# A decoder kernel: the work between the recurrence and block 4, by pairs of batches

## The reference, cut to what matters

```python
# block 3: a gated recurrence, 1024 channels, then a mix back to 256
aiv = x @ W_aiv
a_proj, i_proj, v = jnp.split(aiv, 3, axis=-1)
a = jax.nn.sigmoid(a_proj + decay_bias)
i = jax.nn.sigmoid(i_proj)
input_signal = jnp.sqrt(jnp.maximum(1.0 - a * a, 1e-08)) * (i * v)
h = _chunked_scan(a, input_signal)      # h[t] = a[t] * h[t-1] + input_signal[t]
x = x + h @ W_mix + b_mix
# block 4: cross attention, 16 heads of 16, on a second layer norm
q = _split_heads(query @ Wq.T + bq)     # query = layernorm(x)
scores = jnp.einsum('bhtd,bhsd->bhts', q, k) * scale
attn = jax.nn.softmax(jnp.where(mask[:, None, None, :], scores, -jnp.inf), axis=-1)
out = jnp.einsum('bhts,bhsd->bhtd', attn, v)
x = x + out @ Wo.T + bo
# block 5: one ternary matmul
```

## Time and profile before

| | us |
|---|---|
| median of 3 runs | 472.68 (469.56 to 478.15) |
| profiled execution, its own time | 468.59 |
| its span | 466.8 |
| PE busy | 405.1 |
| DVE busy | 265.4 |
| ACT busy | 162.6 |
| POOL busy | 130.4 |
| aiv projections (L1193) end | 299.7 |
| last state made | 317.3 |
| mix ends | 330.1 |
| first maxima of block 4 | 346.2 |
| first score of batch 0 | 359.8 |
| first score of batch 1 | 370.7 |

### The profile page before, as it was taken

The page is one execution under the profiler, slowest core; times in us unless marked ns, Lnnn a source line. Parts: engine busy times, 40 slices in busy tenths (PEclk is TensorE's granted clock), DMA queues, the critical chain, the costliest instruction groups (busy, mean ns, idle before and its releaser), DMA issues.

```text
span 466.8 us, 7332 instructions
## 1 busy us (share of the span) xinstructions
PE 405.1 (87%) x2920; PEld 266.2 (57%) x2920; DVE 265.4 (57%) x481; ACT 162.6 (35%) x334; POOL 130.4 (28%) x174
## 2 busy tenths in 40 slices
PE   1999977967999986399799999998839999999976
PEld 1556644535467765397555555576513666676655
DVE  5058567996023652012738569985639677677323
ACT  0440530002443133132343554240312566566740
POOL 4720049231763006603550000000162033330100
PEclk9999999986999989589999999999975899999999
DMA  7992003000112796422100000156241333330002
GB/s 232 385 255 92 1 4 93 0 0 1 48 49 69 224 372 276 122 83 62 45 1 0 2 0 0 46 154 159 58 142 53 108 100 98 99 100 2 4 1 70
DMA packets 30616, 42.17 MB, mean 90 GB/s; under 512 B 4330, under 2 KB 27286, under 8 KB 30186
## 3 DMA queue, kind: packets, MB, share of 16 engines
q1 hardware_dynamic: 28279, 35.95, 25.2%
q0 software_dynamic: 2304, 5.76, 4.7%
HBM read 33.00 MB, written 8.98 MB: 90 GB/s over the span
## 4 chain that ended last, share of the span: by engine, by line
PE 67%; DVE 12%; DMA 6%; ACT 5%; POOL 4%; issue 3%; SPq 2%; DVEq 0%; ACTq 0%; POOLq 0%
PE banks L1193 14%; PE banks L951 5%; PE banks L1259 5%; PE banks L1299 4%; PE banks L1006 4%; PE banks L1286 4%; PE banks L991 4%; PE banks L980 3%; PE banks L1227 3%; DVE RA L449 3%; PE banks L940 2%; DMA RC<-NT 2%; PE banks L1031 2%; PE banks L1112 2%; PE banks L1130 2%
## 5 line engine op out<-in xcount | busy, mean ns | idle before, releaser
L1604 DVE TENSOR_REDUCE NM<-banks 100x2 f32<-100x722 f32 x64 | 57.2, 906 | 27.3 <-PE banks L1259 26.2
L1193 PE MATMUL banks<-XT,RBG 128*128 128x400 f32 x192 | 66.7, 510 | 2.1 <-ACT XT L744 2.1
L1193 PEld LDWEIGHTS banks<-XT,RBG 128*128 128x128 f32 x192 | 37.1, 194 | 30.8 <-issue 2.9
L598 POOL TENSOR_TENSOR rstd<-ve,mhalf 100x4 f32<-100x4 f32 x12 | 12.6, 1052 | 140.9 <-DVE ve L1359 140.9
L744 ACT ACTIVATE XT<-banks 128x800 f32<-128x800 f32 x14 | 11.6, 838 | 98.5 <-PE banks L940 98.5
L899 ACT ACTIVATE CT<-banks 128x400 f32<-128x400 f32 (+1 forms) x72 | 35.8, 504 | 26.1 <-PE banks L1286 24.5
L940 PE MATMUL banks<-identf,XN 100*128 100x100 f32 x112 | 15.9, 298 | 19.3 <-DVE XN L1364 9.9
L1259 PE MATMUL banks<-RBG,RC 97*100 97x361 bf16 x64 | 20.9, 425 | 8.1 <-DMA RC<-q_parts 6.6
L1079 PE MATMUL banks<-RC,SELT 128*128 128x400 f32 x64 | 24.6, 534 | 2.7 <-DVE RC L1445 2.4
L940 PEld LDWEIGHTS banks<-identf,XN 100*128 100x128 f32 x112 | 13.8, 169 | 22.6 <-issue 10.6
L1405 DVE TENSOR_TENSOR RC<-RV 128x800 f32<-128x800 f32 x16 | 15.3, 1004 | 17.1 <-ACT RV L786 14.7
(11 more groups left out here) (228 smaller groups left out, 809.6 us busy)
## 6 DMA issues: line engine op xcount, KB each, us to landing
RA<-in_L_ffn_W SPq DMA_DIRECT2D x2, 2048.0 KB, 12.4
k_parts<-RA SPq DMA_DIRECT2D x18, 180.5 KB, 3.4
RBG<-in_L_attn_W_aiv SPq DMA_DIRECT2D x1, 3072.0 KB
CT<-in_ctx_t SPq DMA_DIRECT2D x2, 1444.0 KB, 11.3
RC<-q_parts SPq DMA_DIRECT2D x12, 200.0 KB, 3.7
RBG<-k_parts SPq DMA_DIRECT2D x12, 180.5 KB, 3.6
RA<-k_parts SPq DMA_DIRECT2D x12, 180.5 KB, 3.8
RBG<-k_parts POOLq DMA_DIRECT2D x12, 180.5 KB, 3.7
```

The costliest lines, as they stand in the source:

```text
L1193: ins = mm(PS[2 * aiv_pair(i) + g][:, 0:GC], WA[:, k, c:c + P], XT[:, k, GC * g:GC * g + GC], start=(k == 0), stop=(k == KT - 1))
L1604: v.tensor_reduce(NM[:, b % 2, 2 * i:2 * i + 2], PP[w % 2][0:T, :, 0:S], AX.X, ALU.max, negate=True).then_inc(mx_out, 1)
```

## The change

- **Roots by pairs.** ACT takes roots after every second group; DVE makes a state two groups behind (`inputs(j - 2)`), and two states are left after the loop.
- **The mix by pairs of batches.** A pair's sums lie in one bank. PE runs all eight groups for pair 0, then pair 1 (with pair 0's transposes and query matmuls inside), then pair 2. Pair 3's eight steps (`mix_last`) go into ticks 0 to 14 of block 4.
- **Layer norm, queries, stores and loads by pairs** (`ln_add`, `ln_norm`, `x_tr`, `x_out`, `q_mm`, `q_out`, `queries_through`): pair 0 before block 4, the rest of pairs 1 to 3 in ticks 3 to 26. DVE splits pair 0's queries, POOL those of the other three.
- **Places.** Pair 0's rows lie in RA behind the decays, the other three in RC; SP waits for the whole mix only before these. Query parts and the float32 queries have two buffers each, used in turn.
- The wait of the last squares for old states remains in the text (`u_done, j - 3`), and the semaphores are counted by pair.

The diff, cut to its core (left out: semaphore declarations, counts that follow from them, and the helpers' changed indices):

```diff
-QS = part(RC, 0, G, H, GC, dt=BF16)
+QS = [part(RA, 6500, H, QC, dt=BF16)] + [part(RC, 1600 * i, H, QC, dt=BF16) for i in range(NQ - 1)]
+MIX_BANK = (6, 7, 4, 5)
+TR_BANK = (0, 2, 4, 4)
+Q_BANK = (1, 7, 7, 4)
 P4 = [part(CTF, 1600 * i, H * T) for i in range(3)] + [
     part(SELT[:].rearrange("p a b -> p (a b)"), 0, H * T)]
-QW = part(CTF, 4800, KT, GC)
-QP = part(WX[:].rearrange("p a k d -> p (a k d)"), 0, 3, KT, GC, dt=BF16)
+QW = [part(CTF, 4800 + 400 * i, KT, QC) for i in range(2)]
+QP = [part(WX[:].rearrange("p a k d -> p (a k d)"), 600 * i, 3, KT, QC, dt=BF16) for i in range(2)]
...
+ONCE = ([("mix_last", 2 * j, j) for j in range(RT)]
+        + [("q_mm", 3, 1), ("q_out", 4, 1), ("ln_norm", 5, 2), ("x_tr", 9, 2), ("x_out", 10, 2),
+           ("q_mm", 13, 2), ("q_out", 14, 2), ("ln_add", 15, 3), ("ln_norm", 18, 3), ("x_tr", 23, 3),
+           ("x_out", 24, 3), ("q_mm", 25, 3), ("q_out", 26, 3)])
+ORDER = ("q_mm", "x_tr", "x_out", "q_out", "ln_add", "ln_norm", "parts", "sums_tr", "normalise", "out_tr", "out_mm", "maxima", "scores", "weighted",
+         "os_evac", "add", "mix_last")
...
+            for n, at, x in ONCE:
+                if n == name and name in own and tick == at:
+                    own[name](x)
...
+    def query_ones(p, n):
+        q = QS[p][ROW_MASK:ROW_MASK + 1]
+        if n > 1:
+            q = RC[ROW_MASK:ROW_MASK + 1, 0:1600 * n].bitcast(BF16)
+        else:
+            q = q.rearrange("p h n -> p (h n)")
+        sp.dma_start(q, ones_d.rearrange("a b -> (a b)").unsqueeze(0)[:, 0:H * QC * n]
+                     ).then_inc(qs_one[min(p, 1)], 16)
+    def queries_through(p):
+        sp.wait_ge(q4_first, p + 1)
+        store_queries(p, 0)
+        for i in (1, 2):
+            if p == 0:
+                sp.wait_ge(q4_split, i)
+            else:
+                sp.wait_ge(q4_split1, 2 * (p - 1) + i)
+            store_queries(p, i)
+        for i in range(3):
+            load_queries(sp, p, i)
...
+    query_ones(0, 1)
+    queries_through(0)
     sp.wait_ge(y_mm, 3 * B)
-    sp.dma_start(QS[ROW_MASK:ROW_MASK + 1].rearrange("p g h n -> p (g h n)"),
-                 ones_d.rearrange("a b -> (a b)")[0:H * N].unsqueeze(0)).then_inc(qs_one, 16)
-    for i in range(3):
-        if i == 0:
-            sp.wait_ge(q4_out, 2)
-        else:
-            sp.wait_ge(q4_split, i)
-        store_queries(0, i)
-    for i in range(3):
-        load_queries(sp, 0, i)
+    query_ones(1, NQ - 1)
+    queries_through(1)
     for b in range(B):
         sp.wait_ge(np_out, b + 1)
         for i in range(3):
             load_maxima(sp, b, i)
-        if b == 0:
-            for i in range(3):
-                sp.wait_ge(q4_split1, max(i, 1))
-                store_queries(1, i)
-            for i in range(3):
-                load_queries(sp, 1, i)
+        if b + 2 < NQ:
+            queries_through(b + 2)
...
-    rsqrt(4)
-    pool.wait_ge(q4_out, 4)
-    link(gp.tensor_tensor(QW, QW, QP[:, 0], ALU.subtract))
-    gp.tensor_copy(QP[:, 1], QW).then_inc(q4_split1, 1)
-    pool.wait_ge(q4_split1, 1)
-    gp.tensor_tensor(QP[:, 2], QW, QP[:, 1], ALU.subtract).then_inc(q4_split1, 1)
-    bias(4)
+    def rsqrt_pair(p):
+        pool.wait_ge(var4, p + 1)
+        gp.tensor_tensor(rstd[:, 2 * p:2 * p + 2], ve[:, 2 * p:2 * p + 2], mhalf[:, 0:2], ALU.pow
+                         ).then_inc(rstd4, 1)
+    def split_query(p):
+        qw, qp = QW[p % 2], QP[p % 2]
+        pool.wait_ge(q4_out, p + 1)
+        link(gp.tensor_tensor(qw, qw, qp[:, 0], ALU.subtract))
+        gp.tensor_copy(qp[:, 1], qw).then_inc(q4_split1, 1)
+        pool.wait_ge(q4_split1, 2 * p - 1)
+        gp.tensor_tensor(qp[:, 2], qw, qp[:, 1], ALU.subtract).then_inc(q4_split1, 1)
+    for p in range(3):
+        rsqrt_pair(p)
+    split_query(1)
+    rsqrt_pair(3)
...
+        if b == 0:
+            split_query(2)
+            split_query(3)
+            bias(4)
...
-        if j % 4 == 3:
-            for jj in range(j - 3, j + 1):
+        if j % 2:
+            for jj in (j - 1, j):
...
+    def x_out(p):
+        act.wait_ge(tr4, p + 1)
+        src = PS[TR_BANK[p]][:, 0:KT * QC].rearrange("p (k n) -> p k n", k=KT)
+        sc.activation(XT[:, :, QC * p:QC * p + QC], src, ACT.Copy).then_inc(xt4, 1)
+    def q_out(p):
+        qw, qp = QW[p % 2], QP[p % 2]
+        act.wait_ge(q4_mm, p + 1)
+        if p >= 2:
+            for i in range(3):
+                act.wait_ge(q_st[i], 16 * (p - 1))
+            if p == 2:
+                act.wait_ge(q4_split, 2)
+            else:
+                act.wait_ge(q4_split1, 2 * (p - 2))
+        for m in range(KT):
+            q = PS[Q_BANK[p]][:, QC * m:QC * m + QC]
+            ins = sc.activation(qp[:, 0, m], q, ACT.Identity, bias=BQ4[:, m:m + 1], scale=1 / 4)
+        ins.then_inc(q4_first, 1)
+        for m in range(KT):
+            q = PS[Q_BANK[p]][:, QC * m:QC * m + QC]
+            ins = sc.activation(qw[:, m], q, ACT.Identity, bias=BQ4[:, m:m + 1], scale=1 / 4)
+        ins.then_inc(q4_out, 1)
+    x_out(0)
+    q_out(0)
+    x_out(1)
...
-    pe.wait_ge(iv_done, RT)
-    pe.wait_ge(sig, 2 * RT)
     pe.wait_ge(ld["wmix"], 16)
-    for j in range(RT // 2):
+    def mix(p, j):
         pe.wait_ge(state, j + 1)
-        for b in range(B):
-            mm(PS[b][0:T, 0:D], UU[:, j, b, 1:TP], WMIX[:, j, :], start=(j == 0), stop=False)
-    for b in range(B):
-        for j in range(RT // 2, RT):
-            pe.wait_ge(state, j + 1)
-            ins = mm(PS[b][0:T, 0:D], UU[:, j, b, 1:TP], WMIX[:, j, :], start=False,
-                     stop=(j == RT - 1))
-        ins.then_inc(y_mm, 1)
-    pe.wait_ge(x_new, 3 * B + 6)
-    for i in range(4):
-        g, m = i // 2, i % 2
-        if m == 0:
-            transposes(4 * B, g)
-        pe.wait_ge(xt_ready, 4 * KT * G + KT * (g + 1))
-        if i >= 2:
-            pe.wait_ge(q4_out, i - 1)
-        for k in range(KT):
-            ins = mm(PS[4 + m][:, 0:GC], W4[:, 2, k, m * P:(m + 1) * P], XT[:, k, GC * g:GC * g + GC],
-                     start=(k == 0), stop=(k == KT - 1))
+        for b in (2 * p, 2 * p + 1):
+            ins = mm(PS[MIX_BANK[p]][0:T, b % 2 * D:b % 2 * D + D], UU[:, j, b, 1:TP], WMIX[:, j, :],
+                     start=(j == 0 and b % 2 == 0), stop=(j == RT - 1), skip_group_check=True)
+            if j == RT - 1:
+                ins.then_inc(y_mm, 1)
+    def x_tr(p):
+        if p == 0:
+            pe.wait_ge(sig, 2 * RT)
+        elif p == 1:
+            pe.wait_ge(iv_done, RT)
+        elif p == 3:
+            pe.wait_ge(xt4, 3)
+        for b in (2 * p, 2 * p + 1):
+            pe.wait_ge(xn_ready, 4 * B + b + 1)
+            for k in range(KT):
+                t0 = QC * k + b % 2 * T
+                ins = nc.tensor.transpose(PS[TR_BANK[p]][:, t0:t0 + T], XN[:, b, k * P:(k + 1) * P],
+                                          identf[0:T, 0:T])
+        ins.then_inc(tr4, 1)
+    def q_mm(p):
+        pe.wait_ge(xt4, p + 1)
+        if p == 1:
+            pe.wait_ge(x_new, 3 * B + 4)
+        elif p == 2:
+            pe.wait_ge(q4_out, 2)
+        for m in range(KT):
+            for k in range(KT):
+                ins = mm(PS[Q_BANK[p]][:, QC * m:QC * m + QC], W4[:, 2, k, m * P:(m + 1) * P],
+                         XT[:, k, QC * p:QC * p + QC], start=(k == 0), stop=(k == KT - 1))
         ins.then_inc(q4_mm, 1)
-    pe.wait_ge(x_new, 4 * B)
-    pe.wait_ge(pv_zero, 1)
+    pe.wait_ge(sig, 2 * RT - 1)
+    for j in range(RT):
+        mix(0, j)
+    for j in range(RT):
+        mix(1, j)
+        if j == 4:
+            x_tr(0)
+        if j == 6:
+            q_mm(0)
+    pe.wait_ge(iv_done, RT - 1)
+    for j in range(RT):
+        mix(2, j)
+    x_tr(1)
...
+            pe.wait_ge(q4_out, 3)
...
-        if j >= 4:
-            inputs(j - 4)
+        if j >= 2:
+            inputs(j - 2)
...
-    for j in range(RT - 4, RT):
+    for j in range(RT - 2, RT):
         inputs(j)
-    for b in range(B):
-        add(3, b, PS[b])
-    dve.wait_ge(x_new, 4 * B)
-    dve.wait_ge(q4_out, 2)
-    link(v.tensor_tensor(QW, QW, QP[:, 0], ALU.subtract))
-    v.tensor_copy(QP[:, 1], QW).then_inc(q4_split, 1)
+    def ln_add(p):
+        both = (2 * p, 2 * p + 1)
+        dve.wait_ge(y_mm, 2 * B + 2 * p + 2)
+        if p == 0:
+            dve.wait_ge(bias_added, 3)
+        for b in both:
+            v.tensor_tensor(X[:, b], X[:, b], PS[MIX_BANK[p]][0:T, b % 2 * D:b % 2 * D + D], ALU.add
+                            ).then_inc(x_new, 1)
+        for b in both:
+            stats(4, b)
+        for b in both:
+            aggregate(4, b)
+        dve.wait_ge(aggregated, 4 * B + 2 * p + 2)
+        v.tensor_scalar(ve[:, 2 * p:2 * p + 2], mv[:, 2 * p:2 * p + 2, 1], EPS, None, ALU.add
+                        ).then_inc(var4, 1)
+    def ln_norm(p):
+        dve.wait_ge(rstd4, p + 1)
+        for b in (2 * p, 2 * p + 1):
```

(14 more changed lines are left out.)

86 lines of the change are left out of this document (45 added, 41 removed).

## The result

The changed kernel takes **482.4 us** (median of 4 runs, 481.5 to 486.7) against 472.3 for the kernel before on the same chip (4 runs, 469.6 to 478.2): ratio 1.0235, 95% interval 1.016 to 1.031. The forecast was 468.7, in a range of 462.5 to 474.5, so the prediction was wrong in sign and outside its range.

A forecast was written before the change was run, and what follows sets the result against it. It took PE, busy 87% of the span, as the bound, with slack only in the passage from recurrence into block 4. -6.1 + 1.7 + (0 to 1.9), taken as -4.0, gave 468.7 against the 472.68 median; range 462.5 to 474.5.

The forecast's parts named there:

- States and roots: Recurrence: last state at 310.2 instead of 317.3, 7.1 us earlier; four more table loads covered by the projections.
- The first fall: PE thin from 304.2 to 311.1 during pair 0's mix: half clock afterwards costs 1.7 us.
- Pair 0's queries: Pair 0's layer norm, queries, split and DMA before block 4: first maxima at 329.3 instead of 346.2.
- the row's midpoint: Landing of pair 0's last 100 KB query load: midway between 1.7 and 3.84 us, taken as 2.8.
- The SP rival: Four store and load rounds in SP's queue, 2 us more per store under key loads: 472.7, no change; chance 0.17.
- Pair 3's mix and the first score: Start of block 4: pair 3's mix done at 343.1, first score at 353.1 against 359.8, -6.7 us.
- Batch 0: POOL's splits and bias precede batch 1's maxima: batch 1's first score at 364.6 instead of 370.7, gain 6.1 us.
- the second fall: PE thin from 343.1 to 353.1: half clock doubles pair 3's transposes and query matmuls, 0 to 1.9 us.
- The clock term: Two thin PE stretches, 304.2 to 311.1 and 343.1 to 353.1: +1.7 and 0 to 1.9 us.
- The slower rival: Clock stays low after the first gap, over 10.5 us of fp32 work from pair 0's query wait: 480.7; chance 0.08.
- Within: 0.89: Chance given to a whole-kernel result within 2% (9.5 us) of the kernel before.

The follow-up runs named there:

- e4: Kernel before with only roots by pairs and states two groups behind: ratio 1.0036.
- e1: Changed kernel with POOL's block 4 bias moved behind the split of batch 1's maxima: median 473.8 us.
- e3: Changed kernel with 7 and 6 idle fp32 matmuls before batch 7's last transposes and last output product: median 475.8 us, ratio 1.0134.
- e9: e6's kernel with POOL's key loads issued ahead of the split of the maxima: median 464.5 us, ratio 0.980.
- e2: Changed kernel with 28 small idle fp32 matmuls on PE right before its wait for batch 1's split maxima: median 478.8 us.
- e8: e7 plus two idle fp32 matmuls of 400 columns ahead of each of pair 0's mix steps 6 and 7: ratio 0.998, median of all 475.1 us.
- e12: Kernel before with 7 repeated copies (2.0 us) on POOL ahead of batch 3's split of the maxima: 475.5 us, ratio 1.005.
- e7: e6's kernel plus 22 idle fp32 matmuls ahead of PE's wait before the first score: median 478.7 us, ratio 1.012.
- e10: Kernel before with POOL's key loads issued ahead of the split of the maxima: ratio 0.999.
- e6: Changed kernel with the edits of e1 and e3 together: median 471.3 us of six runs, ratio 0.986.

## Why the prediction was wrong, point by point

- **States and roots: right.** The last state ended at 310.80 (310.2 forecast), and the loads cost nothing (e4). PE waited 0.78, 1.66 and 0.74 us for states, and the last step of pair 0 began at 310.84.
- **The first fall: right in place and size.** Clock 0.50 from 308 to 312; PE's 24 records from 310.84 on took 7.16 us, where 20 had taken 4.48 at full clock: 1.8 us more, 1.7 forecast.
- **Pair 0's queries: 2.7 us too early.** First maxima at 331.98, not 329.3. The chain shows the reason:

```profile
322.24 4.14 DMA q_parts<-WX
326.40 0.59 SPq L430
...
329.57 2.27 DMA RA<-q_parts
```

  The store took 4.14 us from ScalarE's result until the loads could go, while the key loads still kept the DMA engines 0.76 busy (322 to 326); I had given split, issue and landing together 2.0. The landing of the last load (2.27, forecast 2.8) was well bounded: of the two readings, the row's midpoint was too high by 0.5. The other, the estimate of 2.9 from the fixed cost of a DMA in the Trainium skill (DMA: Bandwidth & Descriptors, "Anatomy of one DMA"), was too high by 0.6. The SP rival had this mechanism, but 2 us are its whole part.
- **Pair 3's mix and the first score: 2.5 us late in all.** Last mix step to 344.6 (343.1), first score at 355.61 (353.1). The gain there was 4.2 instead of 6.7.
- **Batch 0, the step that failed.** I had the wait: "adds the bias, 4.49 us, all ahead of batch 1's maxima", through at 360.7; it was 363.57, as pair 3's mix ended 1.5 us late and the second fall, which I had in the sum, slowed its queries. I priced it as a wait, the difference between 364.6 and 362, and went on at full clock: "After that the order is the old one." What came was a stop of 2.90 us, then 24 us at half clock. Batch 1's first score stood at 371.16, 6.6 us behind the forecast (2.9 from POOL, 3.7 from PE's now slow way from the split to the score), and its sums 21.9 us after that instead of 14.6 before. e1 shows what the wait is worth: without it 10 us come back in the profile, and 8.6 in the median of all runs (482.4 to 473.8, with 472.3 and 473.5 for the kernel before beside them). It is not the only thing that can start this fall (e3, e9).
- **The clock term.** I looked for falls in the two stretches that are thin *because of the change's mix*, found both (308 to 315, 348 to 355) and priced each by the work *inside* the thin stretch, 1.7 and 0 to 1.9 us. The third thin place, PE's idle time from 360.7 to 363.6, I had worked out myself (362 to 364.6 at the score) and didn't put into this list. And a fall is priced by what is behind it until the clock is back: 24 us of block-4 work, half of it lost, 12 us against my forecast at full clock.
- **The slower rival was the right mechanism in the wrong place.** It kept the clock low on the moved fp32 matmuls, 327.6 to 338, and gave 480.7; there the clock stayed at 1.00. It stayed low on block 4's matmuls behind the bias instead. My argument against it, "packed fp32 matmuls brought it back within 3.5 us", is true of such matmuls (e2: back within 3 us of the fill's start). It doesn't carry over to block 4's mix of small ones, behind which the clock was back after 7 us in e2, e8 and e12, but after 17 in e7 and 27 here. The row that did say it was in my hands: 345 to 365 at 0.50 with PE 17.32 of 20 us busy. I used it as the rival's price and gave it 0.08.
- **The steady part and the tail: not in the forecast.** +1.5 us from PE's three waits for the maxima rows (2.0 us), which go away with the key loads out of their way (e9). Why they are longer than before's one wait of 0.54 us, with the same loads in the same order, is open: the landings were 4.2 to 4.4 us against 3.9 to 4.1. +4.3 us from a fall at 461, at waits that before has too; e4 has it as well, and e10 and e12 in part. That fall is a matter of the execution, not of the change alone: nothing in these runs ties it to the change.
- **The scatter.** "Within: 0.89" rested on it that the change can do no more than its small sum. A kernel whose clock hangs on a wait has a lever far larger than the wait.

**Settled:** the loss is PE's clock, 29 us more at half rate than in the kernel before (51.2 against 21.8), at half a microsecond each: 3.4 us before 344, 6.9 between 344 and 440 and 4.5 in the tail, 14.7 in all, where the span grew by 13.6; the wait for the bias is one thing that starts the long fall, and all four runs without it (e1) are faster than all four with it; and the pairs with that wait gone, the tail filled and the key loads moved beat the kernel before (0.980). The key loads alone do nothing for the kernel before (0.999), and the first two edits without them are not shown to beat it (e6). The tail's fill was not tried in the kernel before, whose profile has almost none there; e4's and those of e10 to e12 have one, so part of the gain may be had without the pairs. **Open:** how often the waits at the first two scores start the long fall with the bias out of the way; why a stop of 0.9 to 1.3 us is followed by a fall in one execution and not in another; what a clean stop of 3 us does in the steady part.

## What to carry to other kernels

Where a change brings PE idle time of a microsecond or more, price not the wait alone but also the chance that the work behind it runs at half clock, up to where a trace showed the clock come back on *that kind* of work: here 7 to 27 us of small bf16 and fp32 matmuls against 3 us of wide fp32 ones. List every idle place that your own sum produces, also those that another engine's queue makes, and ask of a long in-order operation (the 4.5 us bias) whose result is needed first. In the result, compare PE's busy time before all else: if it grows without added work, it is the clock.

## What was not expected of the hardware

- PE 24.00 of 24 us busy at half clock, three times (the changed kernel and e9 from 364, e3 from 362), and 16 of 16 in e7. The Trainium skill (TensorE: Matmul & The Clock Gate, "What's actually happening") calls the half rate the default state and says that activity releases it. These rows don't agree, as 24 us without a gap did not release it, while e2's fp32 fill does (0.50 at 358 to 362, 1.00 from 365).
- One program, executed again, gets its falls at other places or not at all: e9 from 461.2 to 474.2 us, with a mean granted clock between 0.956 and 0.924. The section of the Trainium skill just named says that the number of matmuls at the half rate at a kernel's start varies from run to run. No row here is of the start; in these runs the falls inside the kernel vary.
- Idle matmuls for 6.25 us were cheaper than a wait of 2.9 (e2), yet with idle matmuls at another place the fall came elsewhere (e7, ratio 1.012).
- A 3 KB load landed in 1.7 us alone and in 4.1 to 5.0 behind six key loads of 180 KB; with those issued ahead of the split it was 1.7 to 2.6 again (e9, e10).
- The number of packets under 512 bytes went from 4330 to 7691 with the query rows at half length, at the same 42.17 MB, and the query loads, of 100 KB now, landed in 2.4 to 2.6 us (medians of the four rounds), where those of 200 KB had taken 3.7.
